# Scatters of routed rows regrouped around the second attention, and rows of the last three tiles in buffers of their own

## The reference, cut to what matters

```python
x = x + cross_attention(layernorm(x), ctx, ctx)       # 16 x 64 rows against 16 x 512 keys
x = x + self_attention(layernorm(x))                  # 16 heads of 32, rotary positions
x = x + moe(layernorm(x))                             # the part that matters here

def moe(x):                                           # E = 8 experts, 2048 hidden
    logits = xf @ Wr + br
    thresh = top_k(logits, 2)[:, 1:2]
    weights = softmax(where(logits >= thresh, logits, -inf))
    h = gelu(xf @ W1[e] + b1[e]); expert_out = h @ W2[e] + b2[e]
    return sum_e weights[:, e] * expert_out
```

## Time and profile before

| | us |
|---|---|
| median of 3 runs | 1745.26 (1740.12 to 1748.06) |
| the profiled execution | 1732.61, of which the span 1730.8 |
| PE busy in it | 1647.2 (95%) |
| DVE, ACT, POOL busy | 879.5, 695.6, 306.7 |
| second attention's steps with scatters, one per row tile | 17.3 each |

### The profile page before, as it was taken

One profiled execution on the slowest core, in us unless ns is written; L12 is line 12 of the kernel. 1 busy time (PEld: TensorE's weight loads), 2 busy tenths in 40 slices (PEclk: granted clock), 3 DMA queues, 4 the chain that ended last, 5 costly groups with the idle time before them and its releaser, 6 DMA issues. The chain is left out here.

```text
span 1730.8 us, 26944 instructions
## 1 busy us (share of the span) xinstructions
PE 1647.2 (95%) x10858; PEld 1388.6 (80%) x10858; DVE 879.5 (51%) x1592; ACT 695.6 (40%) x1314; POOL 306.7 (18%) x258
## 2 busy tenths in 40 slices
PE   7999999999999999999999987996799999999987
PEld 6888888888888888888888775774688889889876
DVE  4344434443344344343443565786668548549852
ACT  5333333333333333333332433444556337336531
POOL 3201210111001110111010051456411002102101
PEclk9999999999999999999999998997799999999889
DMA  6601830111011101110102451113747428528711
GB/s 223 219 16 53 127 79 7 53 56 53 7 53 56 53 8 52 56 53 17 43 7 77 147 187 35 52 52 101 256 140 234 147 86 242 160 88 238 217 47 21
DMA packets 54101, 165.16 MB, mean 95 GB/s; under 512 B 10612, under 2 KB 10996, under 8 KB 53408
## 3 DMA queue, kind: packets, MB, share of 16 engines
q1 hardware_dynamic: 38032, 131.88, 22.3%
q0 software_dynamic: 15920, 31.19, 8.7%
HBM read 143.54 MB, written 55.64 MB: 115 GB/s over the span
## 5 line engine op out<-in xcount | busy, mean ns | idle before, releaser
L407 PE MATMUL psum<-ctx,Wk 128*128 128x512 f32 x1536 | 384.9, 399 | 0.0
L407 PE MATMUL psum<-Wv,ctx 128*128 128x512 f32 x1536 | 368.7, 389 | 0.0
L407 PEld LDWEIGHTS psum<-Wv,ctx 128*128 128x128 f32 x1536 | 288.4, 188 | 59.9
L407 PEld LDWEIGHTS psum<-ctx,Wk 128*128 128x128 f32 x1536 | 279.2, 188 | 55.5
L912 DVE SCALAR_TENSOR_TENSOR kT<-psum,bkc,kT 128x512 fp32r<-128x512 f32 x128 | 96.0, 750 | 387.7 <-ACT kT L1278 387.7
L407 PE MATMUL psum<-xgT,Wh 128*128 128x224 f32 (+5 forms) x1536 | 251.5, 317 | 12.2 <-issue 9.1
L407 PEld LDWEIGHTS psum<-xgT,Wh 128*128 128x128 f32 x1536 | 229.4, 197 | 30.6 <-issue 12.6
L750 PE MATMUL psum<-Wh,hs 128*128 128x512 f32 x981 | 246.7, 397 | 0.0
L750 PEld LDWEIGHTS psum<-Wh,hs 128*128 128x128 f32 x981 | 181.7, 191 | 34.1 <-DVE hs L1166 0.3
L1278 ACT ACTIVATE kT<-psum,bkc 128x512 fp32r<-128x512 f32 x128 | 88.3, 690 | 247.7 <-PE psum L407 247.6
L1443 ACT ACTIVATE gl<-psum,b1c 128x512 f32<-128x512 f32 x128 | 87.8, 687 | 202.5 <-PE psum L407 202.4
(11 more groups left out here) (149 smaller groups left out, 1784.2 us busy)
## 6 DMA issues: line engine op xcount, KB each, us to landing
raw<-in_W SPq DMA_DIRECT2D x128, 512.0 KB, 3.9
expert_rows<-in_spare_rows SPq DMA_DIRECT2D x16, 1042.0 KB, 7.7
raw<-in_ctxT SPq DMA_DIRECT2D x32, 512.0 KB, 4.3
xg<-expert_rows POOLq DMA_DIRECT2D x32, 256.0 KB, 5.4
low_parts<-Olo POOLq DMA_DIRECT2D x32, 128.0 KB, 2.4
oT<-low_parts SPq DMA_DIRECT2D x8, 512.0 KB, 4.4
out_x<-x SPq DMA_DIRECT2D x12, 256.0 KB, 2.2
xs<-in_x SPq DMA_DIRECT2D x4, 512.0 KB, 6.7
```

What stands on the lines that cost most here:

```text
L407: mm = pe.matmul(dst, l, r, start=n == 0, stop=n == len(pairs) - 1)
```

## The change

POOL's scatters of tile i-3 in steps 3 to 7 are now issued as experts 0 and 1, the power, experts 2 to 4, the wait for o2_psum, experts 5 to 7, and the bias. Before it was 2, 4 and 2. Tiles 5, 6 and 7 have buffers of their own in a region that the projections of tiles 0 to 4 have left by then, so `norm_x2` of these tiles waits for those projections only, and the first Gelu and `slot_left(13)` no longer wait for tiles 6 and 7. POOL's order after step 7 is now: (5, 0 to 2), power(6), a wait for the logits of tile 6, (5, 3 to 4), (6, 0), power(7), (5, 5), (7, 0), `fetch_rows(0)`, and behind it 16 scatters: (5, 6 to 7), (6, 1 to 7), (7, 1 to 7). All 64 scatters stay.

```diff
+        LATE = NT - 3
+        nx2 += [place(f"nx2{3 + r}", c0 + 16 + 4 * r, [P, ROW]) for r in range(NT - LATE)]
         def sent(t):
-            return 16 * E * (t // 3 + 1) - (16 if t >= NT - 2 else 0)
+            return 16 * E * (t // 3 + 1) - (16 if t >= LATE else 0)
+        def x2_rows(t):
+            return nx2[t % 3 if t < LATE else 3 + t - LATE]
...
             def norm_x2(t):
-                if t >= 3:
+                if t >= LATE:
+                    v.wait_ge(qkv_psum, 3 * LATE)
+                elif t >= 3:
...
                 elif i == 13:
-                    s.wait_ge(rows_sent[(NT - 1) % 3], sent(NT - 1))
+                    s.wait_ge(rows_sent[(LATE - 1) % 3], sent(LATE - 1))
...
-                    if n == 0:
-                        s.wait_ge(rows_sent[(NT - 2) % 3], sent(NT - 2))
...
             for i in range(NT + 2):
                 if 3 <= i < NT:
                     send_rows(i - 3, range(0, 2))
+                elif i == NT:
+                    send_rows(LATE, range(0, 3))
                 if d_on(i, 2):
                     power(...)
-                if d_on(i, 3):
-                    if i < NT:
-                        send_rows(i - 3, range(2, 6))
-                        g.wait_ge(o2_psum, i)
-                        send_rows(i - 3, range(6, E))
-                    elif i == NT:
-                        send_rows(i - 3, range(E))
-                    else:
-                        for e_ in range(1, 6):
-                            send_row(NT - 2, e_, rows_sent[(NT - 2) % 3])
-                if i == NT:
-                    g.wait_ge(slot_step, 3 * (NT - 1))
-                    send_row(NT - 2, 0, first_sent)
+                if 3 <= i < NT:
+                    send_rows(i - 3, range(2, 5))
+                    g.wait_ge(o2_psum, i)
+                    send_rows(i - 3, range(5, E))
+                elif i == NT:
+                    g.wait_ge(lg_psum, NT - 1)
+                    send_rows(LATE, range(3, 5))
+                    send_rows(NT - 2, range(0, 1))
+                elif i == NT + 1:
+                    send_rows(LATE, range(5, 6))
+                    send_rows(NT - 1, range(0, 1))
...
-            g.wait_ge(slot_step, 3 * NT)
-            send_row(NT - 1, 0, first_sent)
             fetch_rows(0)
-            for e_ in range(6, E):
-                send_row(NT - 2, e_, rows_sent[(NT - 2) % 3])
-            for e_ in range(1, E):
-                send_row(NT - 1, e_, rows_sent[(NT - 1) % 3])
+            send_rows(LATE, range(6, E))
+            send_rows(NT - 2, range(1, E))
+            send_rows(NT - 1, range(1, E))
```

More of the change, by code:

```diff
@@ L632, in turn_x2 @@
                     pe.wait_ge(slot_step, 3 * t)
-                transposes(bank[7], [nx2[t % 3][:, k * P:(k + 1) * P] for k in range(KD)]).then_inc(x2T_psum, 1)
+                transposes(bank[7], [x2_rows(t)[:, k * P:(k + 1) * P] for k in range(KD)]).then_inc(x2T_psum, 1)
             def logits(t):
@@ L1026, in route @@
                 lg, top, ex, sm = (rt[:, i, :] for i in range(4))
-                tail = nx2[t % 3][:, D:D + META]
+                tail = x2_rows(t)[:, D:D + META]
                 first = 9 * t
@@ L1084, in norm_x2 @@
                 v.wait_ge(x2_pow, t + 1)
-                if t >= 3:
+                if t >= LATE:
+                    v.wait_ge(qkv_psum, 3 * LATE)
+                elif t >= 3:
                     v.wait_ge(x2T_psum, t - 2)
                     v.wait_ge(rows_sent[t % 3], sent(t - 3))
-                v.tensor_scalar(nx2[t % 3][:, 0:D], x1[:, t, :], mv2[:, ring, 0:1], rstd2[:, ring, 0:1], ALU.subtract, ALU.mult).then_inc(e_norm, 1)
+                v.tensor_scalar(x2_rows(t)[:, 0:D], x1[:, t, :], mv2[:, ring, 0:1], rstd2[:, ring, 0:1], ALU.subtract, ALU.mult).then_inc(e_norm, 1)
             def o2_low(t):
@@ L1537, in send_row @@
             def send_row(t, e_, sent_on):
-                g.indirect_dma_start(lists, bass.IndirectOffsetOnAxis(slot[:, t, e_:e_ + 1], 0), nx2[t % 3][:], None,
+                g.indirect_dma_start(lists, bass.IndirectOffsetOnAxis(slot[:, t, e_:e_ + 1], 0), x2_rows(t)[:], None,
                                      bounds_check=SLOTS - 1, oob_is_err=False).then_inc(sent_on, 16)
@@ L1547, in send_rows @@
                 for e_ in experts:
-                    send_row(t, e_, rows_sent[t % 3])
+                    send_row(t, e_, first_sent if t >= LATE and e_ == 0 else rows_sent[t % 3])
             g.wait_ge(x1_done, NT)
@@ L1580, in fetch_rows @@
                 if q == 0:
-                    g.wait_ge(rows_sent[(NT - 3) % 3], sent(NT - 3))
-                    g.wait_ge(first_sent, 32)
+                    for t in range(LATE - 3, LATE):
+                        g.wait_ge(rows_sent[t % 3], sent(t))
+                    g.wait_ge(first_sent, 16 * (NT - LATE))
                     g.wait_ge(out_seeded, SEEDS)
@@ L1585, in fetch_rows @@
                 else:
-                    for t in range(NT - 2, NT):
+                    for t in range(LATE, NT):
                         g.wait_ge(rows_sent[t % 3], sent(t))
```

## The result

| | median us | runs |
|---|---|---|
| before | 1746.66 | 6, 1740.12 to 1753.58 |
| after | 1733.3 | 6, 1726.63 to 1735.2 |

The ratio is 0.9922, with a 95% interval of 0.9903 to 0.9942: the change makes the kernel faster by 13.4 us. The forecast was 1744.8 and no change that could be told, with a range of 1738.5 to 1751. The median of before now has three more runs than the 1745.26 above.

What follows compares the result with a forecast made beforehand. PE, busy for 95% of the span, was taken as the bound. The terms 0 + 0.55 - 0.39 - 0.3 - 0.4 = -0.5 us, carried to the median of 1745.26, gave 1744.8 us, range 1738.5 to 1751.

Steps and rivals of the forecast that it cites:

- That lies 12.65 us under the median; I carry the difference over.: Whole kernel: profiled execution of 1732.61 us against the median; the -0.5 us sum applied to 1745.26 gives 1744.8.
- Five tiles, 0 us.: Steps 3 to 7: the regrouping moves the bias back 1.28 us, and DVE waits for PE's scores anyway: 0 us.
- the steps of 17.3 us changed their length: Second attention: a sign that the prediction would be wrong; no size given.
- the late power(6): Last step: three scatters go before power(6), so norm(6) and PE's transposition slide: +0.55 us, bounds 0 and +1.2.
- The held `nm`: Last step: DVE's first `nm` held by POOL's bias until 1181.15, 0.1 us gained and absorbed; not held, up to 1.6.
- (7, 0) and its landing: Before expert 0: the scatter starts 0.78 after its places, -0.39 us; its landing and the fetch, -0.3 us.
- The -0.3: Landing of (7, 0): -0.4 us with five scatters gone, +0.1 for the fetch sharing time with weight loads.
- Behind the fetch: Sixteen scatters in place of nine take 22.9 us; `fetch_rows(1)` starts at 1244.3, 10 us later, hidden with 3.9 to spare.
- The slower rival: Scatters beside the experts cost up to 2.27 us each, expert 1's rows come late: +9.0 us, 1754.3; chance 0.10.
- ACT's wait of 3.16 us: Expert 0: ACT's wait for a weight load issued together with the fetch, expected gone or halved.
- PE's 0.47 us: Start of expert 0: PE idle until a Gelu; with the fetch later, -0.4 us, bounds 0 and -0.47.
- The tail gains: Rival: `nm` slips past the bias, power(6) costs nothing, (7, 0) lands like an idle one: -4.4 us, 1740.9; chance 0.15.

Runs made afterwards that it cites:

- again: The kernel before once more, nothing changed: 1744.91 us, ratio 0.9991 (chip 10).
- scores: The kernel after, but in the last step the scatters of experts 5 to 7 wait for s2_psum, not o2_psum: 1730.48 us, ratio 1.0001 (chip 9).
- power: As scores, with power(6) after two of tile 5's scatters, the third moved behind the wait for the logits: 1731.13 us, ratio 1.0001 (chip 9).
- plain: The kernel after with one plain 64 KB DMA by POOL in steps 3 to 7, just ahead of the products: 1731.34 us, ratio 1.0001 (chip 9).
- groups: The kernel before with only the regrouping of steps 3 to 7 to 2, 3 and 3 scatters: 1736.54 us, ratio 0.9933 (chip 10).
- plain2: The plain kernel again, on chip 14: 1731.23 us, ratio 0.9989.
- power3: The power kernel a third time, on chip 15: 1733.25 us, ratio 0.9920.
- early3: The kernel before without POOL's wait for o2_psum in steps 3 to 7, so six scatters in one run, third run: 1770.03 us, ratio 1.0127 (chip 15).
- tail: The kernel after with the old grouping of 2, 4 and 2 back in steps 3 to 7: 1739.20 us, ratio 0.9957 (chip 10).

## Why the prediction was wrong

**The step that failed is the scale.** "That lies 12.65 us under the median; I carry the difference over." The difference was not a constant of the measurement. It was the loss itself: the profile shows an execution in which scatters over small products are free, the median comes from executions in which they cost some 15 us up to the fetched rows (again, 145.86 against 130.80), 11.5 of it within the blocks. The change takes 12.4 us of that away. On chips of the profile's kind the kernel before takes 1731 to 1733 us, in line with its 1732.61, and the kernel after is neither faster nor slower there as far as its near relatives tell (scores and power, 1.0001 each; plain, 0.9989 to 1.0006). The kernel after itself was not timed on such a chip.

**"Five tiles, 0 us."** The regrouping was priced by the bias and by POOL's order. For the profiled execution 0 is right (steps 2 to 7 take 86.29 us there and 86.20 to 86.27 in plain). In the timed ones it is -4.8 us in these steps and -7.7 up to the fetched rows (groups against again): expert 5's scatter leaves the 64 products. The prediction had named it as a sign of being wrong if the steps of 17.3 us changed their length; they were 18.5 us in again and 17.3 in the kernel after. What I did not price was that a scatter and PE's products meet at all. The first profile had that scatter over the block too, without any trace of a cost.

**Step 8.** +0.55 us for the late power(6). PE's transposition waited 1.34 us for DVE's norm in the kernel after and started 16.25 us after step 7's products, in before 13.71 (1188.13 from this start):

```profile
1174.42 0.86 PE L681 MATMUL psum<-PT,vn 64*32 64x64 f32 x64
```

Of these 2.54 us the gaps in the scores are 1.78. In plain, without such gaps, it started after 14.50: 0.79 us later than in before. Right in mechanism and near in size. What counts is the other thing in this step: tile 5's scatters left the block of products, 6.66 us to 1.18.

**The held `nm`.** The score block of the kernel after has gaps, so I read this in plain2, whose POOL order around the bias is the same and whose score block is whole: POOL's bias ran from 1178.13 for 1.33 us. The timeline of DVE there:

```profile
1177.91 0.69 DVE L1019 TENSOR_REDUCE mx<-psum 128x8 f32<-128x512 f32 x1 [0.48 <-PE psum L615]
1178.63 0.86 DVE L1021 TENSOR_SCALAR nm<-mx 128x8 f32<-128x8 f32 x1
1179.41 0.68 DVE L1019 TENSOR_REDUCE mx<-psum 128x8 f32<-128x512 f32 x1
1180.12 0.17 DVE L1021 TENSOR_SCALAR nm<-mx 128x8 f32<-128x8 f32 x1
```

The first `nm` takes 0.86 us in place of 0.17 and ends at 1179.49, just after the bias (1179.46); the reduction that started under it took its usual 0.69. Held, as forecast, if for half as long, since the scores and `nm` fell later against the bias. By this row the rule of the Trainium skill (SBUF — State Buffer, Who interferes with whom) holds. In the steady steps the products of 128x8 are free of the bias: L1050 of the kernel after takes 0.17 us at 1141.40, by DVE's timeline.

**(7, 0) and its landing.** The places were ready at 1207.38 + 0.17 and the scatter started at 1208.33, 0.78 later, as said. The fetch started 4.48 us after the scatter's issue ended, against 4.28, though the issue itself took 1.35 us in place of 0.98: from its start 5.83 against 5.26. The -0.3 was wrong in sign, by 0.9 us.

**Behind the fetch.** The sixteen scatters took 24.0 us, not 22.9, and `fetch_rows(1)` started at 1246.80 (1244.3 forecast); PE turned the rows at 1255.57 without a wait. The slower rival stayed where it was put. ACT's wait of 3.16 us became 0.70 and PE's 0.47 us went, as forecast. What that was worth the profiles can't tell: from the first transposition to that of expert 1's rows it is 37.88 us in before and 36.19 in after, and 36.5 to 39.7 in the other profiles with the old order.

So the terms that could be checked within the profile's own kind of execution were within 1 us, and the sum was about an execution without the loss, while the median was set by executions with it. "The tail gains" came out in sign, for a reason that it did not contain.

## What to carry to other kernels

A profiled execution that lies outside the spread of the timed runs is not a sample of them: find out what it lacks before carrying a difference over, and profile the kernel before again, on another chip too. Compare starts in two profiles only from a common point just ahead of the place in question. Keep POOL's indirect DMAs off dense blocks of small matrix products; power3, with its scatters in groups between such blocks, has no gap in them on a chip with the loss, where one scatter over 64 products costs 1.2 us (again), three cost 4.3 (early3) and a run of them 5.5 (again) to 6.3 (groups). An idle time whose end the profile puts down to "issue", in the middle of a block of equal instructions, is a mark of it.

## What the runs showed of the hardware that was not expected

Chips differ in this. On two of the six numbered ones (10 and 15) PE runs 41 to 44 small products in one piece (41 or 42 in 0.66 to 0.68 us; 44 score products in 1.2, slower than the 64 in 1.16 elsewhere) and is then fed in pieces, mostly of four or five, while POOL issues scatters and for up to 1.0 us behind them. Behind the first, the pieces start 0.69 to 0.77 us apart or 1.4 to 1.5 us, not at the scatters' 1.29. Then the rest goes through at once. On the other four (0, 9, 13, 14) PE isn't held up at all. The kernel before takes 1747 and 1748 us on the first two and 1731 to 1733 on the others. The first 40 or so pass in each block, as if a store of instructions ahead of PE ran dry; that is a guess, and what it is, and what differs between the chips, no run here shows.

POOL's bias addition over the scores does not do it (groups), and packets on their way don't either. Blocks of 12 large products under scatters show no gap: in the kernel after they take 1.74 to 1.83 us, 0.15 us for each product, beside the sixteen scatters and behind them alike, where the small ones take 0.013 us each. Behind a starved block the products could pay a second time: the clock was 0.59 behind a block of 5.17 us, and behind blocks of 2.0 to 2.3 us it was 1.00 in steps 3 to 6 of again, but 0.58 in its step 7, and 0.72 in one step of tail.
